# Mixture inputs as 128 and 64 rows, nine passes an expert, the inner remainder on POOL and row normalisation on ACT, in a vision transformer layer

## The chip, the cores and the metric

One core of one Trainium2 chip runs the whole program. Its engines are TensorE (PE), VectorE (DVE), ScalarE (ACT), GpSimd (POOL) and SyncE (SP, which only issues DMAs here); each takes its instructions in the order in which they are written, and engines wait for each other on semaphores. The metric is the device time of one execution in microseconds; smaller is better.

## The reference

The program is one layer of a vision transformer on 64 images of 3 x 224 x 224. Patch embedding gives 197 tokens of 192 features an image. Then comes attention with a residual, and then a mixture of experts with a residual, which is the part that the change touches:

```python
h = tok(x)                                   # 64 x 197 x 192
h = h + attn(layernorm(h))
y = layernorm(h)                             # rows of 192
scores = sigmoid(y @ gate_weight.T)          # 8 experts in 4 groups
# the best 2 groups, then the best 2 experts in them; their scores, normalised, are the weights cw
h1, h3 = y @ w1[e].T, y @ w3[e].T            # 192 -> 128, for each expert e
out = h + sum_e cw[e] * (silu(h1) * h3) @ w2[e].T + shared expert of the same shape
```

All 8 experts are computed for all tokens, with weight nought where an expert isn't chosen, and the shared expert is a ninth.

## The kernel before

The kernel has a set-up block and two phases. The set-up block loads the weights, and splits each into a high and a low part of 16 bits (`hi`, `lo`). Products use three passes, hi x hi, lo x hi and hi x lo, and leave lo x lo out. Phase A (embedding and attention) writes its tokens to DRAM; it isn't touched by the change.

Phase B is the mixture. It takes 12608 tokens in groups of 512 (4 lanes of 128 rows): 24 full groups and one of 320 (4 lanes of 80). For a group, `stats_of` (DVE) makes mean and variance of each row, `rstds` (POOL) the reciprocal square root, `normalise` (DVE) writes `bnorm`, `transposes` (PE) turn it into `ps_x`, `yT_out` splits it into `yT_hi` (ACT) and `yT_lo` (DVE), `gate` (PE) makes the scores, and `route` (DVE, five parts of small dependent steps) the weights `comb`. The 192 features lie as two chunks of 96 rows.

For each of the nine experts e of a group:

- `inner_products` (PE): for w1 and w3, two chunks and three passes of 512 columns, 12 matmuls, into `ps_h1` and `ps_h3` (two buffers each).
- `silu` (ACT) of ps_h1 into `act1`; `multiply` (DVE) by ps_h3 into `inner`; `inner_first` (ACT) rounds to `in_hi`; `inner_rest` (DVE) gives `in_lo` = inner - in_hi.
- `outer_products` (PE): 12 matmuls of 192 columns into `ps_y`, in two halves; each half waits until `accumulate` has read that half of the expert before, and the first waits for `in_lo`.
- `accumulate` (DVE) adds comb x ps_y to `acc`, four instructions (two for the shared expert, L1130).

The order is written out by hand. PE issues the inner products of e, then the outer products of e-2; after expert 3's it does the transposes of the following group, after expert 5's that group's gate. DVE issues multiply(e), inner_rest(e-1), accumulate(e-2), and then: routing parts 3 and 4 of the own group behind experts 0 and 1; of the following group `stats_of` behind 1, `normalise` behind 2, `yT_out` behind 4, routing parts 0 to 2 behind 6, 7 and 8. ACT issues silu(e), inner_first(e), and the following group's `yT_out` behind 3 and `gate_out` behind 5. POOL does only `rstds`, once a group. SP loads the group after the next and stores this one. `run` unrolls three groups, loops over pairs, and unrolls the last four.

PE's outer products of expert 0 thus stand behind the inner products of expert 2, and need in_lo(0) and the accumulation of the shared expert of the group before.

## Time and profile before

| | us |
|---|---|
| median of 3 runs | 2052.69 (2049.91 to 2053.3) |
| the profiled execution's own time | 2049.82 |
| its span, first to last instruction | 2047.9 |
| PE busy | 1920.0 (94%) |
| DVE busy | 1319.4 (64%) |
| ACT busy | 909.9 (44%) |
| POOL busy | 47.4 (2%) |
| mean granted TensorE clock | 0.982 |

The busy times are of the whole span; phase A takes the first half, phase B begins near 1116 us. PE's busy time overlaps its weight loads, and a matmul's record is longer than the time after which the next can start, so issue times are taken from start to start.

### The profile page before, as it was taken

How to read it: one execution, taken by the hardware profiler on the slowest of the kernel's cores; microseconds unless marked ns; L12 is line 12 of the kernel's file. 1: busy time of each engine (PE TensorE's matmuls, PEld its weight loads, DVE VectorE, ACT ScalarE, POOL GpSimd, SP SyncE). 2: the span in 40 equal slices, each digit the busy share in tenths (PEclk: the TensorE clock that was granted, in tenths of full speed). 3: DMA queues.
4: the chain of work that ended last, by engine and by line, in shares of the span. 5: the costliest groups of instructions: out<-in, count | busy, mean ns of one | idle time of the engine just before them, and what ended most of it. 6: DMA issues, size and time to landing. Idle time of an engine off the chain costs nothing. (4 is left out here: it accounts for less than half of the span.)

```text
span 2047.9 us, 47882 instructions
## 1 busy us (share of the span) xinstructions
PE 1920.0 (94%) x17848; PEld 1348.0 (66%) x17848; DVE 1319.4 (64%) x3554; ACT 909.9 (44%) x1878; POOL 47.4 (2%) x63
## 2 busy tenths in 40 slices
PE   3999999999999999999996999999999999999998
PEld 2777777777777777777774555555555555555556
DVE  3455545455454554544452888888888888888887
ACT  2555555555555555555553333333333333333332
POOL 0000000000000000000000000000000000000000
PEclk9999999999999999999996999999999999999999
DMA  4011111111111111111100000000000000000000
GB/s 152 17 46 50 57 47 46 48 46 46 48 46 47 47 59 35 55 53 47 46 23 28 17 24 17 31 15 15 31 15 23 23 15 31 15 23 23 16 21 14
DMA packets 31508, 74.73 MB, mean 36 GB/s; under 512 B 3435, under 2 KB 16366, under 8 KB 31214
## 3 DMA queue, kind: packets, MB, share of 16 engines
q1 hardware_dynamic: 31310, 72.10, 11.3%
q8 instruction: 123, 2.02, 0.4%
q14 instruction: 75, 0.61, 0.1%
HBM read 52.73 MB, written 19.37 MB: 35 GB/s over the span
## 5 line engine op out<-in xcount | busy, mean ns | idle before, releaser
L572 ACT ACTIVATE prob<-ps_sc 99x792 f32<-99x792 f32 x384 | 317.4, 827 | 109.4 <-PE ps_sc L413 90.8
L907 PE MATMUL ps_h<-yT_hi,w_hi 96*128 96x512 f16 (+1 forms) x900 | 341.2, 379 | 0.0
L909 PE MATMUL ps_h<-yT_lo,w_hi 96*128 96x512 f16 (+1 forms) x900 | 339.9, 378 | 0.0
L910 PE MATMUL ps_h<-yT_hi,w_lo 96*128 96x512 f16 (+1 forms) x900 | 339.7, 377 | 0.0
L357 PE MATMUL ps_hid<-lin_f,xin 128*99 128x192 f32 x1536 | 288.6, 332 | 32.5 <-DMA xin<-xp 29.2
L981 ACT ACTIVATE in_hi<-inner 128x512 f16<-128x512 f32 (+1 forms) x225 | 140.4, 624 | 337.9 <-DVE inner L1100 337.9
L357 PEld LDWEIGHTS ps_hid<-lin_f,xin 128*99 128x99 f32 x1536 | 243.3, 170 | 34.4 <-DMA xin<-xp 29.2
L925 PE MATMUL ps_y<-w_hi,in_hi 128*128 128x192 f16 (+1 forms) x900 | 222.3, 247 | 39.6 <-DVE acc L1124 28.0
L973 ACT ACTIVATE act<-ps_h 128x512 f32<-128x512 f32 (+1 forms) x225 | 132.3, 588 | 274.7 <-PE ps_h L910 274.0
L1124 DVE SCALAR_TENSOR_TENSOR acc<-ps_y,comb,acc 128x192 f32<-128x192 f32 (+1 forms) x700 | 242.3, 407 | 0.0
L1100 DVE SCALAR_TENSOR_TENSOR inner<-ps_h,act 128x512 f32<-128x512 f32 (+1 forms) x225 | 152.4, 677 | 125.4 <-ACT act L973 115.5
L927 PE MATMUL ps_y<-w_hi,in_lo 128*128 128x192 f16 (+1 forms) x900 | 221.1, 246 | 0.0
L926 PE MATMUL ps_y<-w_lo,in_hi 128*128 128x192 f16 (+1 forms) x900 | 220.9, 245 | 0.0
L413 PE MATMUL ps_sc<-qT,kT 32*99 32x198 f32 x3072 | 180.3, 349 | 6.4 <-DVE kT L676 1.8
L428 PE MATMUL ps_o<-prob,v 98*32 98x198 f32 (+1 forms) x3072 | 172.0, 342 | 12.5 <-ACT prob L572 8.1
L910 PEld LDWEIGHTS ps_h<-yT_hi,w_lo 96*128 96x128 f16 x900 | 88.1, 98 | 105.7 <-issue 3.2
L1106 DVE TENSOR_TENSOR in_lo<-inner,in_hi 128x512 f16<-128x512 f32 (+1 forms) x225 | 151.2, 672 | 0.0
L658 DVE TENSOR_REDUCE qk_var<-qk_sq 99x24 f32<-99x384 f32 x128 | 70.2, 549 | 125.2 <-ACT qk_sq L531 125.2
L925 PEld LDWEIGHTS ps_y<-w_hi,in_hi 128*128 128x128 f16 (+1 forms) x900 | 88.2, 98 | 90.9 <-DVE acc L1124 33.8
L413 PEld LDWEIGHTS ps_sc<-qT,kT 32*99 32x99 f32 x3072 | 116.4, 161 | 42.9 <-issue 16.3
L909 PEld LDWEIGHTS ps_h<-yT_lo,w_hi 96*128 96x128 f16 x900 | 88.7, 99 | 79.5 <-issue 1.9
L907 PEld LDWEIGHTS ps_h<-yT_hi,w_hi 96*128 96x128 f16 x900 | 88.2, 98 | 79.3 <-issue 2.4
(112 smaller groups left out, 3001.0 us busy)
## 6 DMA issues: line engine op xcount, KB each, us to landing
xin<-xp SPq DMA_DIRECT2D x64, 594.0 KB, 3.9
hidden_dram<-h SPq DMA_DIRECT2D x64, 147.0 KB
hin<-hidden_dram SPq DMA_DIRECT2D x24, 384.0 KB, 3.0
out<-acc SPq DMA_DIRECT2D x24, 384.0 KB, 2.3
w_f<-w SPq DMA_DIRECT2D x1, 1728.0 KB, 11.7
hidden_dram<-h SPq DMA_DIRECT2D x64, 0.8 KB
w_f<-w SPq DMA_DIRECT2D x1, 864.0 KB, 13.2
lin_f<-w_lin SPq DMA_DIRECT2D x1, 576.0 KB
```

The source lines that it names most:

```text
L357: last = pe.matmul(hid[:, t, :], xin[q][:, k, t * TR:(t + 1) * TR], lin_f[:, k, :], start=(k == 0), stop=(k == PCHUNKS - 1))
L413: last = pe.matmul(sc[:, place, m, :], kT[p][rows, quad, m * TR:(m + 1) * TR], qT[p][rows, quad, :], start=True, stop=True)
L428: last = pe.matmul(o_quad[VB * place:VB * place + VB, :], v[p][rows, m, QUAD * quad + place, :], prob[quad][rows, place, m, :], start=(m = ...
L572: act.activation(prob[quad][:, places].rearrange("p h m s -> p h (m s)"), ps_sc[0:TR, places, 0:2 * SLOTS], ACT.Exp, scale=D ** -0.5 / (SQ ...
L907: pe.matmul(bank[:, 0:N], w13_hi[:, k, e, w, :], yT_hi[p][:, k, 0:N], start=(k == 0), stop=False)
L909: pe.matmul(bank[:, 0:N], w13_hi[:, k, e, w, :], yT_lo[p][:, k, 0:N], start=False, stop=False)
L910: last = pe.matmul(bank[:, 0:N], w13_lo[:, k, e, w, :], yT_hi[p][:, k, 0:N], start=False, stop=(k == 1))
L925: pe.matmul(dst, in_hi[b][:, s], w2_hi[:, e, :], start=True, stop=False)
L926: pe.matmul(dst, in_hi[b][:, s], w2_lo[:, e, :], start=False, stop=False)
L927: last = pe.matmul(dst, in_lo[b][:, s], w2_hi[:, e, :], start=False, stop=True)
L1100: dve.scalar_tensor_tensor(out=inner[e % 3][:, 0:N], in0=ps_h3[b][:, 0:N], scalar=SA / SS, in1=act1[b][:, 0:N], op0=ALU.mult, op1=ALU.mult ...
L1124: last = dve.scalar_tensor_tensor(out=acc[p][0:R, t, :], in0=ps_y[half_no][0:R, u * C:(u + 1) * C], scalar=comb[p][0:R, t, e:e + 1], in1=b ...
```

## The change

- The 192 features of `yT_hi` and `yT_lo` lie as one chunk of 128 rows and one of 64. The 64 are held twice, in rows 0 to 63 and 64 to 127 of chunk 1. The host lays out w13 and the gate's weights alike (`tailed`).
- In chunk 1, rows 0 to 63 of `w13_hi` hold the high part and rows 64 to 127 the low part. One full matmul w13_hi x yT_hi on 128 rows makes hi x hi and lo x hi at once. The remaining hi x lo pass needs only 64 rows; `w13_lo` has the high part in rows 0 to 63 for w1 and in rows 64 to 127 for w3. So an expert has 2 x 4 full matmuls and two of 64 rows, on different rows of the array and into different banks.
- The gate has five matmuls a lane, where it had six.
- `inner_rest` goes from DVE to POOL, and waits for the silu of the next expert as well. In POOL's body, the following group's `rstds` come ahead of the remainder of expert 0.
- `normalise` goes from DVE to ACT, as eight activations a group with a scale and a bias for each row; `bnorm` is 256 wide, features 128 to 191 twice. Its two halves stand behind experts 1 and 2. POOL makes the bias from mean and reciprocal root, by two more instructions.
- `stats_of` moves from behind expert 1 to behind expert 0.
- In the set-up block w13 grows from 96 to 128 rows, and its low part is made by four instructions where it was one (the gate's too).

```diff
 # set-up block, DVE
+                        if f in tailed:
+                            dve.scalar_tensor_tensor(out=lo[:, 0], in0=f[:, 0], scalar=SW, in1=hi[:, 0],
+                                                     op0=ALU.mult, op1=ALU.subtract)
+                            dve.tensor_copy(lo[0:64, 1], hi[0:64, 1])
+                            dve.memset(lo[64:128, 1], 0.0)
+                            dve.scalar_tensor_tensor(out=hi[64:128, 1], in0=f[64:128, 1], scalar=SW, ...
+                        elif f is w13_f:
+                            dve.scalar_tensor_tensor(out=lo[:, 0], in0=f[:, 0], scalar=SW, in1=hi[:, 0], ...
+                            dve.tensor_copy(lo[0:64, 1, :, 0, :], hi[0:64, 1, :, 0, :])
+                            dve.tensor_copy(lo[64:128, 1, :, 1, :], hi[64:128, 1, :, 1, :]).then_inc(w_tail_done, 1)
+                            dve.wait_ge(w_tail_done, 1)
+                            dve.scalar_tensor_tensor(out=hi[64:128, 1], in0=f[64:128, 1], scalar=SW, ...
 # PE
             def transposes(g):
-                pe.wait_ge(bnorm_done, g.times(1, 1))
+                pe.wait_ge(bnorm_done, g.times(2, 2))
...
-                for k in range(2):
-                    for t in range(T):
-                        last = pe.transpose(ps_x[k][0:KC, t * R:(t + 1) * R], bnorm[0:R, t, k * KC:(k + 1) * KC],
-                                            id32[0:R, 0:R])
+                for t in range(T):
+                    s = slice(t * R, (t + 1) * R)
+                    for k in range(2):
+                        last = pe.transpose(ps_x[k][:, s], bnorm[0:R, t, k * 128:(k + 1) * 128], id32[0:R, 0:R])
             def gate(g):
...
-                    for k in range(2):
-                        pe.matmul(dst, yT_hi[p][:, k, s], gate_hi[:, k, :], start=(k == 0), stop=False)
-                        pe.matmul(dst, yT_hi[p][:, k, s], gate_lo[:, k, :], start=False, stop=False)
-                        last = pe.matmul(dst, yT_lo[p][:, k, s], gate_hi[:, k, :], start=False, stop=(k == 1))
+                    pe.matmul(dst, yT_hi[p][:, 0, s], gate_hi[:, 0], start=True, stop=False)
+                    pe.matmul(dst, yT_hi[p][:, 0, s], gate_lo[:, 0], start=False, stop=False)
+                    pe.matmul(dst, yT_lo[p][:, 0, s], gate_hi[:, 0], start=False, stop=False)
+                    pe.matmul(dst, yT_hi[p][:, 1, s], gate_hi[:, 1], start=False, stop=False)
+                    last = pe.matmul(dst, yT_lo[p][:, 1, s], gate_lo[:, 1], start=False, stop=True)
             def inner_products(g, e):
...
-                for w, bank in ((0, ps_h1[b]), (1, ps_h3[b])):
-                    for k in range(2):
-                        pe.matmul(bank[:, 0:N], w13_hi[:, k, e, w, :], yT_hi[p][:, k, 0:N],
-                                  start=(k == 0), stop=False)
-                        pe.matmul(bank[:, 0:N], w13_hi[:, k, e, w, :], yT_lo[p][:, k, 0:N], start=False, stop=False)
-                        last = pe.matmul(bank[:, 0:N], w13_lo[:, k, e, w, :], yT_hi[p][:, k, 0:N],
-                                         start=False, stop=(k == 1))
+                for w, bank in enumerate(banks):
+                    pe.matmul(bank, w13_hi[:, 0, e, w, :], y_hi[:, 0], start=True, stop=False)
+                    pe.matmul(bank, w13_hi[:, 0, e, w, :], y_lo[:, 0], start=False, stop=False)
+                    pe.matmul(bank, w13_lo[:, 0, e, w, :], y_hi[:, 0], start=False, stop=False)
+                    pe.matmul(bank, w13_hi[:, 1, e, w, :], y_hi[:, 1], start=False, stop=False)
+                for w, bank in enumerate(banks):
+                    rows = slice(64 * w, 64 * w + 64)
+                    last = pe.matmul(bank, w13_lo[rows, 1, e, w, :], y_lo[rows, 1], start=False, stop=True)
 # ACT
+            def normalise(g, half_no):
+                R, p = rows_of(g), g.mod(2)
+                act.wait_ge(bneg_done, g.times(1, 1))
+                if half_no == 0 and reached(g.times(1)):
+                    act.wait_ge(yT_done, g.times(1))
+                for t in (2 * half_no, 2 * half_no + 1):
+                    for dst, src in ((slice(0, C), slice(0, C)), (slice(C, 256), slice(128, C))):
+                        last = act.activation(bnorm[0:R, t, dst], hin[p][0:R, t, src], ACT.Identity,
+                                              scale=brstd[0:R, t:t + 1], bias=bshift[0:R, t:t + 1])
+                last.then_inc(bnorm_done, 1)
...
                     inner_first(g, e)
+                    if e in (1, 2) and following.active():
+                        normalise(following, e - 1)
 # DVE
                     multiply(g, e)
-                    if e > 0:
-                        inner_rest(g, e - 1)
-                    elif g.back(1).active():
-                        inner_rest(g.back(1), NE - 1)
...
                     if following.active():
-                        if e == 1:
+                        if e == 0:
                             stats_of(following)
-                        if e == 2:
-                            normalise(following)
 # POOL
                 pool.tensor_tensor(brstd[0:R], bvareps[0:R], minus_half[0:R], ALU.pow).then_inc(brstd_done, 1)
+                pool.wait_ge(brstd_done, g.times(1, 1))
+                settle(pool, settled)
+                pool.tensor_tensor(bshift[0:R], bmv[0:R, :, 0], brstd[0:R], ALU.mult).then_inc(bshift_done, 1)
+                pool.wait_ge(bshift_done, g.times(1, 1))
+                settle(pool, settled)
+                pool.tensor_scalar(bshift[0:R], bshift[0:R], -1.0, None, ALU.mult).then_inc(bneg_done, 1)
+            def inner_rest(g, e):
+                N, b = T * rows_of(g), e % 3
+                pool.wait_ge(inhi_done, g.times(NE, e + 1))
+                if e + 1 < NE or g.back(-1).active():
+                    pool.wait_ge(silu_done, g.times(NE, e + 2))
+                settle(pool, settled)
+                pool.tensor_tensor(in_lo[b][:, 0:N], inner[b][:, 0:N], in_hi[b][:, 0:N],
+                                   ALU.subtract).then_inc(inlo_done, 1)
...
             def body(g):
-                if g.back(-1).active():
-                    rstds(g.back(-1))
+                for e in range(NE):
+                    if e == 0 and g.back(-1).active():
+                        rstds(g.back(-1))
+                    inner_rest(g, e)
```

## Rows read from the trace of the kernel before

**Rows 1.** Windows, phase B: us, busy PE, PEld, DVE, ACT, POOL; clock, DMA.

```profile
1400.00:1600.00 200.00, 188.28 (x1341) 112.41 (x1342) 167.16 (x468) 64.50 (x114) 9.63 (x11) 0.98 0.06 22
```

**Rows 2.** The timeline of POOL, phase B: start, us, what, idle before.

```profile
1437.08 0.23 POOL L1179 TENSOR_SCALAR bvareps<-bmv 128x4 f32<-128x4 f32 x1 [36.39 <-DVE bmv L1010]
1437.39 1.56 POOL L1181 TENSOR_TENSOR brstd<-bvareps,minus_half 128x4 f32<-128x4 f32 x1
...
1991.00 0.22 POOL L1179 TENSOR_SCALAR bvareps<-bmv 80x4 f32<-80x4 f32 x1 [34.34 <-DVE bmv L1010]
```

**Rows 3.** The timeline of PE, one group of tokens; columns as before.

```profile
1426.27 0.25 PE L925 MATMUL ps_y<-w_hi,in_hi 128*128 128x192 f16 x1
...
1427.26 0.38 PE L907 MATMUL ps_h<-yT_hi,w_hi 96*128 96x512 f16 x1
...
1429.86 0.25 PE L925 MATMUL ps_y<-w_hi,in_hi 128*128 128x192 f16 x1
...
1433.93 0.26 PE L925 MATMUL ps_y<-w_hi,in_hi 128*128 128x192 f16 x1 [0.33 <-DVE acc L1130]
...
1438.77 0.26 PE L925 MATMUL ps_y<-w_hi,in_hi 128*128 128x192 f16 x1 [1.08 <-DVE acc L1124]
...
1440.58 1.08 PE L880 MATMUL ps_x<-id,bnorm 128*96 128x128 f32 x8 [0.49 <-DVE bnorm L1019]
```

**Rows 4.** The timeline of DVE in the same stretch.

```profile
1419.93 0.69 DVE L1100 SCALAR_TENSOR_TENSOR inner<-ps_h,act 128x512 f32<-128x512 f32 x1 [0.47 <-ACT act L973]
...
1423.76 0.69 DVE L1100 SCALAR_TENSOR_TENSOR inner<-ps_h,act 128x512 f32<-128x512 f32 x1 [0.20 <-DVE rank L1061]
...
1427.29 0.69 DVE L1100 SCALAR_TENSOR_TENSOR inner<-ps_h,act 128x512 f32<-128x512 f32 x1 [0.20 <-DVE masked L1080]
...
1428.50 1.39 DVE L1124 SCALAR_TENSOR_TENSOR acc<-ps_y,comb,acc 128x192 f32<-128x192 f32 x4
1429.80 0.41 DVE L1052 TENSOR_TENSOR cmp<-masked 128x256 f32<-128x256 f32 x1
...
1432.12 0.69 DVE L1100 SCALAR_TENSOR_TENSOR inner<-ps_h,act 128x512 f32<-128x512 f32 x1 [0.20 <-DVE rank L1061]
...
1433.33 1.01 DVE L1130 SCALAR_TENSOR_TENSOR acc<-ps_y,acc 128x384 f32<-128x384 f32 x2
...
1435.22 1.13 DVE L1006 BATCH_NORM_STATS2 bstats<-hin 128x6 f32<-128x192 f32 x4
```

**Rows 5.** The timeline of ACT, one expert.

```profile
1426.47 0.60 ACT L973 ACTIVATE act<-ps_h 128x512 f32<-128x512 f32 x1 [1.19 <-PE ps_h L910]
1428.10 0.63 ACT L981 ACTIVATE in_hi<-inner 128x512 f16<-128x512 f32 x1 [1.03 <-DVE inner L1100]
```

**Rows 6.** Timeline of PE, phase A: from full matmuls to 32-row ones.

```profile
613.63 0.25 PE L342 MATMUL ps_mix<-proj_hi,onT_lo 96*99 96x192 f16 x1
613.80 0.93 PE L413 MATMUL ps_sc<-qT,kT 32*99 32x198 f32 x16
614.66 0.37 PE L428 MATMUL ps_o<-prob,v 98*32 98x198 f32 x3
```

**Rows 7.** Grouped lines of ACT by shape: count, busy us, mean ns, idle.

```profile
L543 ACT ACTIVATE qk_lnvar<-qk_var,eps_qk 99x24 f32<-99x24 f32 x128 | 40.2, 314 | 91.6 <-DVE qk_var L658 91.6
...
L546 ACT ACTIVATE qk_rstd<-qk_lnvar 99x24 f32<-99x24 f32 x128 | 28.5, 223 | 4.1
```

**Rows 8.** The timeline of POOL in the first microseconds.

```profile
0.83 1.41 POOL L226 MEMSET qk_norm<- 99x768 f32 x2
```

**Rows 9.** The timeline of PE around the gating products.

```profile
1412.33 0.17 PE L892 MATMUL ps_x<-gate_hi,yT_hi 96*128 96x8 f16 x1
...
1412.93 0.38 PE L907 MATMUL ps_h<-yT_hi,w_hi 96*128 96x512 f16 x1
```

**Rows 10.** The windows view over four microseconds at the low clock.

```profile
1402.00:1406.00 4.00, 3.61 (x13) 2.28 (x14) 2.76 (x7) 1.71 (x3) 0.00 (x0) 0.57 0.33 98
```

**Rows 11.** The timeline of DVE in the set-up block.

```profile
17.95 6.82 DVE L217 SCALAR_TENSOR_TENSOR w_lo<-w_f,w_hi 96x4608 f16<-96x4608 f32 x2 [6.44 <-ACT w_hi L199]
```

More of the change, by code:

```diff
@@ L123, in vit_layer @@
             proj_hi, proj_lo = split_pair("proj", [KC, 2, C])
-            gate_hi, gate_lo = split_pair("gate", [KC, 2, EXPERTS])
-            w13_hi, w13_lo = split_pair("w13", [KC, 2, NE, 2, INTER])
+            gate_hi, gate_lo = split_pair("gate", [128, 2, EXPERTS])
+            w13_hi, w13_lo = split_pair("w13", [128, 2, NE, 2, INTER])
             w2_hi, w2_lo = split_pair("w2", [INTER, NE, C])
@@ L216, in _ @@
                         dve.wait_ge(w_hi_done, n + 1)
-                        dve.scalar_tensor_tensor(out=lo[:], in0=f[:], scalar=SW, in1=hi[:],
-                                                 op0=ALU.mult, op1=ALU.subtract).then_inc(w_lo_done, 1)
+                        if f in tailed:
[3 more added lines that the diff above has]
+                            dve.memset(lo[64:128, 1], 0.0)
+                            dve.scalar_tensor_tensor(out=hi[64:128, 1], in0=f[64:128, 1], scalar=SW,
+                                                     in1=hi[64:128, 1], op0=ALU.mult,
+                                                     op1=ALU.subtract).then_inc(w_lo_done, 1)
+                        elif f is w13_f:
+                            dve.scalar_tensor_tensor(out=lo[:, 0], in0=f[:, 0], scalar=SW, in1=hi[:, 0],
+                                                     op0=ALU.mult, op1=ALU.subtract)
+                            dve.tensor_copy(lo[0:64, 1, :, 0, :], hi[0:64, 1, :, 0, :])
+                            dve.tensor_copy(lo[64:128, 1, :, 1, :], hi[64:128, 1, :, 1, :]).then_inc(w_tail_done, 1)
+                            dve.wait_ge(w_tail_done, 1)
+                            dve.scalar_tensor_tensor(out=hi[64:128, 1], in0=f[64:128, 1], scalar=SW,
+                                                     in1=hi[64:128, 1], op0=ALU.mult,
+                                                     op1=ALU.subtract).then_inc(w_lo_done, 1)
+                        else:
+                            dve.scalar_tensor_tensor(out=lo[:], in0=f[:], scalar=SW, in1=hi[:],
+                                                     op0=ALU.mult, op1=ALU.subtract).then_inc(w_lo_done, 1)
                 @block.gpsimd
@@ L769, in phase_b @@
         brstd = sb("brstd", [128, T])
-        bnorm = sb("bnorm", [128, T, C])
-        yT_hi = [sb(f"yT_hi{p}", [KC, 2, GT], F16) for p in range(2)]
-        yT_lo = [sb(f"yT_lo{p}", [KC, 2, GT], F16) for p in range(2)]
+        bshift = sb("bshift", [128, T])
+        bnorm = sb("bnorm", [128, T, 256])
+        yT_hi = [sb(f"yT_hi{p}", [128, 2, GT], F16) for p in range(2)]
+        yT_lo = [sb(f"yT_lo{p}", [128, 2, GT], F16) for p in range(2)]
         act1 = [sb(f"act1{p}", [INTER, GT]) for p in range(2)]
@@ L956, in yT_out @@
                 for k in range(2):
-                    act.activation(yT_hi[p][:, k, 0:N], ps_x[k][0:KC, 0:N], ACT.Copy,
+                    act.activation(yT_hi[p][:, k, 0:N], ps_x[k][:, 0:N], ACT.Copy,
                                    scale=SX).then_inc(yThi_done, 1)
@@ L983, in _ @@
             first = Index(0, 0, 2, GROUPS_B)
+            normalise(first, 0)
+            normalise(first, 1)
             yT_out(first)
@@ L1010, in stats_of @@
                     dve.bn_aggr(bmv[0:R, t, :], bstats[0:R, t, :]).then_inc(bmv_done, 1)
-            def normalise(g):
-                R, p = rows_of(g), g.mod(2)
-                dve.wait_ge(brstd_done, g.times(1, 1))
-                if reached(g.times(1)):
-                    dve.wait_ge(yT_done, g.times(1))
-                for t in range(T):
-                    last = dve.tensor_scalar(bnorm[0:R, t, :], hin[p][0:R, t, :], bmv[0:R, t, 0:1],
-                                             brstd[0:R, t:t + 1], ALU.subtract, ALU.mult)
-                last.then_inc(bnorm_done, 1)
             def yT_out(g):
@@ L1026, in yT_out @@
                     dve.wait_ge(yThi_done, g.times(2, k + 1))
-                    dve.scalar_tensor_tensor(out=yT_lo[p][:, k, 0:N], in0=ps_x[k][0:KC, 0:N], scalar=SX,
+                    dve.scalar_tensor_tensor(out=yT_lo[p][:, k, 0:N], in0=ps_x[k][:, 0:N], scalar=SX,
                                              in1=yT_hi[p][:, k, 0:N], op0=ALU.mult,
@@ L1101, in multiply @@
                                          in1=act1[b][:, 0:N], op0=ALU.mult, op1=ALU.mult).then_inc(mul_done, 1)
-            def inner_rest(g, e):
-                N, b = T * rows_of(g), e % 3
-                dve.wait_ge(inhi_done, g.times(NE, e + 1))
-                dve.tensor_tensor(in_lo[b][:, 0:N], inner[b][:, 0:N], in_hi[b][:, 0:N],
-                                  ALU.subtract).then_inc(inlo_done, 1)
             def accumulate(g, e):
@@ L1136, in _ @@
             stats_of(first)
-            normalise(first)
             yT_out(first)
```

19 lines of the change are left out of this document (13 added, 6 removed).

## The prediction

> **What bounds the kernel now.** I read the windows view first. In phase B a 200-us stretch has PE busy for 188 and DVE for 167, at a granted clock of 0.98, while ACT has 64.5 and POOL under 10 [rows 1]. PE is nearly full and DVE is close behind; the reader should ask where each ends the wait. The timeline of POOL gives the length of one group of 512 tokens, because its reciprocal square root runs once a group: 1437.08 to 1991.00 us is 15 groups, 36.93 us each [rows 2]. The timelines of PE and DVE then show one group from inside. An expert's outer products take 0.99 us of issue (1426.27 to 1427.26) and its inner products 2.60 (to 1429.86), so PE needs 3.59 an expert [rows 3]. It stalls in three places of the group, always for DVE: 0.33 for the shared expert's accumulation, 1.08 for the next one, 0.49 for the normalised rows ahead of the transposes [rows 3]. They follow experts 0 and 1, where DVE has the large routing part (1429.80 to 1432.12, 2.32 us) and the statistics (from 1435.22) on top of its usual work [rows 4]. So PE's columns bound most of a group, and DVE's queue bounds the stretch around experts 0 to 3. Phase A is not touched.
>
> **The sum, part by part.** I number the experts of a group 0 to 8 and write P(e) for the moment at which PE has issued the inner products of expert e. The method is to walk one group queue by queue. Checked on the kernel before: PE's outer products of expert 0 need the first half of the shared expert's accumulation, which starts at 1433.33 and takes 0.5; PE starts at 1433.93 [rows 3, 4]. The walk holds there to 0.1 us.
>
> *Nine passes.* Twelve 512-column matmuls took 2.60, 0.216 each [rows 3]. Eight remain full, and two use 64 rows each, on different rows and banks. Phase A shows such packing: 16 matmuls of 32 rows take 0.86 us (613.80 to 614.66), 0.054 each, against 0.082 for one 192-column matmul of the outer products (0.99/12), so they overlap; going in costs 0.17 minus 0.08, 0.09 [rows 3, 6]. I price the pair at 0.216, plus 0.09, plus about 0.07 for its stagger and the way out (bounds 0 and 0.3 for the three together): 2.10 for the inner products, 3.09 for an expert's step. The transposes' weights grow from 96 to 128 columns: between 1.08 [rows 3] and 4/3 of it, I take 1.25. The gate's 24 products took 0.60 [rows 9]; 20 take 0.50.
>
> *The inner remainder moves to POOL.* DVE loses one of two equal halves of 1428.50 minus 1427.29, 0.60 an expert [rows 4]. POOL gains it. No long POOL subtraction is in the trace. From below it is DVE's 0.60; a memset of 768 elements takes about 0.70, so two input streams of 512 take 0.93, with 0.23 for a tiny operation 1.1, and with a third stream for the output 1.6 [rows 2, 8]. I take 1.1. The Trainium skill, GPSIMD Engine Reference, section 3.1, puts two-input arithmetic at 2.6 cycles an element at 1.2 GHz, and calls ordinary elementwise work the wrong use of this engine; that would be an estimated 1.11 plus dispatch, and the sum would stay. In a usual step it is hidden: silu(e+1) starts 0.20 behind P(e+1) and takes 0.60 [rows 3, 5], so POOL ends near P(e+1)+1.95, and PE wants the result only at P(e+2), that is P(e+1)+3.09. Above 2.2 us the cover is gone.
>
> *Row normalisation on ACT.* DVE loses four instructions a group, and PE its 0.49 wait. ACT gains eight. A 24-element one takes 0.22, an operand per row adds 0.09 [rows 7], and the slope to the 0.60 of 512 elements [rows 5] gives, with two such operands, 0.53 for 192 and 0.43 for 64 elements: 1.9 a half group, less what back-to-back instructions overlap. I take 1.6 (bounds 1.4 and 1.9). ACT has 135 of 200 us free [rows 1]. In experts 1 and 2 silu stands behind it; the walk below shows whether that hurts.
>
> *The queue of POOL.* This is the step I weigh most. In a group's body POOL first issues the next group's rstds, and only then the remainder of expert 0. The rstds wait for the statistics, which now stand at the end of DVE's expert 0. Behind them wait in_lo(0), then PE's outer products of expert 0, then all of PE. Walk from P(0)=0. silu(0) ends and DVE's multiply starts at 0.82; the accumulation at 1.42 and takes 1.30 (1428.50 to 1429.80), so routing starts at 2.72, and 2.32 later, at 5.04, the statistics [rows 4]. POOL's first instruction follows the start of the statistics by 1.86 (1435.22 to 1437.08): 6.90 [rows 2, 4]. It and the power take 1.87 (0.31 and 1.56); the two added small ones, each with its wait, 0.31 each: 9.39 [rows 2]. in_lo(0) ends at 10.54, and PE can go on at 10.64. PE itself is there at P(2)=6.18. **A new stall of 4.5 us replaces the 1.9 of before.**
>
> *The rest of the group.* P(3)=13.73. ACT normalises until 11.0, silu(2) ends at 11.6, in_lo(1) at 12.8: in time for 13.73. The second half ends near 14.65, the transposes are due at 14.72: in time, 0.6 late at worst. in_lo(2) ends near 16.4 against P(4)=18.07. Later DVE is the shorter queue: the step from multiply 7 to multiply 8 was 3.83 and becomes 3.23, that to the next group's 3.53 becomes 2.93 [rows 4], against 3.09 of PE; the 0.14 over is absorbed. So after 10.64 PE issues seven outer sets (6.93), seven inner sets (14.70), the transposes (1.25) and the gate (0.50): the period is 34.0.
>
> *The clock.* After such stalls the granted clock fell in places: 1402 to 1406 ran at 0.57, with PE at the lower of its two levels (1.2 instead of 2.4 GHz) for most of it [rows 10]. That is 43% of 4 us, 1.7 lost. The 0.98 of the long stretch is 4 us lost in 200, so two such falls in some five groups [rows 1, 2]; their cost is in the 36.93. With PE idle for 4.5 us in a row in every group I expect one such fall in each; part of it lies in the idle time, some last longer: 1.6 a group (bounds 0 and 3.3). Period 35.6.
>
> *Sum.* 36.93 minus 35.6 is 1.3 us, times 24 periods, 32 us. Once only: the larger first and second matrices in the set-up block, where two DVE instructions took 6.82 [rows 11] and three more come, with a third more bytes ahead of them, cost 2 to 5, I take 3.5; the first group's normalisation has nothing to hide under: ACT's 3.2 and POOL's 0.62 for DVE's 1.2, 2.5; the short last group gains some 2. Net 4. So 28 us off. Against its own profiled time of 2049.8 that is 2021.8; the median of the runs is 2.9 above that execution, so I forecast **2025**. Anything within 0.2% (4 us) of 2052.7 is what a measurement can't tell from no change.
>
> **Rivals.**
> 1. *The clock holds* through the stalls, as in most groups of before. Period 34.0: 2.9 times 24, less 4, gives 1987. Against: the stalls of before were 0.3 to 1.1 long, this one 4.5 [rows 3].
> 2. *The POOL queue doesn't bind,* since DVE is ready earlier or POOL's chain is shorter beside other work. PE then waits only for the shared expert's accumulation, near 7.8: period 31.2, 1920. Against: the power alone takes 1.56 [rows 2].
> 3. *On the other side: POOL and DVE block each other.* The subtraction runs beside multiply and accumulate. If each holds DVE for its whole 1.1, expert 0 ends 1.1 later, and four other steps that carry routing or yT_lo run over by about 0.8: 4.3 a group, 2128. From 0.3 us of blocking an instruction on the kernel is slower. For: nothing in the trace has a long POOL operation beside DVE. Against: the power ran beside multiply, and DVE's spacing stood [rows 2, 4], though it reads four elements. The Trainium skill, SBUF — State Buffer, "Who interferes with whom", lets only DVE instructions with two SBUF inputs (or in a two-port mode) collide with a reading POOL; here DVE reads PSUM and one SBUF operand, so by that rule the blocking is nought where in_lo runs.
> 4. *The low clock lasts twice as long* in each group: 1.7 more, 2066.
> 5. *The pair does not overlap,* ten passes and not nine: seven times 0.216, 1.5 a group, 2061. Against: rows 6.
>
> **How the numbers follow.** Main case 0.54, with 2004 to 2045 as its own range (the bounds of clock, pair and subtraction each moving it by part of their width); rival 1 0.14, rival 2 0.08, rival 3 0.09, rival 4 0.08, rival 5 0.07. Range 1980 to 2066: it leaves out rival 2, rival 3 and little else. Faster 0.75, same 0.03, slower 0.22.
>
> **What would show it.** One long idle stretch of PE in each group, ahead of the outer products of expert 0, released by POOL's in_lo; POOL starts about 34 to 36 us apart; the step of PE near 3.09; the subtraction near 1.1; DVE under 0.75 busy; ACT near 75 of 200 us; the granted clock of phase B near 0.95. The forecast is wrong if the stall is short or split, if the subtraction or DVE's instructions stretch when they meet, or if the clock stays at 1.00.

## The result and the profile after

The changed kernel takes 2020.7 us (median; 2018.69 to 2022.14) against 2052.5 for the kernel before (2049.91 to 2053.3) on the same chip: ratio 0.9852, 95% interval 0.9831 to 0.9873. So it is 32 us, 1.5%, faster, which is clear of the noise. The forecast was 2025. The profiled execution spans 2019.0 us.

The page shows where to look first, in its parts 4 and 5: a wait of TensorE for POOL, which the kernel before did not have. Columns of a group: line, engine, operation, operands, count; busy us, mean ns; idle us just before and what ended most of it.

```profile
PE 28%; DVE 8%; POOL 3%; issue 3%; ACT 1%; DVEq 0%; POOLq 0%; DMA 0%; ACTq 0%
...
L1215 POOL TENSOR_TENSOR in_lo<-inner,in_hi 128x512 f16<-128x512 f32 (+1 forms) x225 | 257.9, 1146 | 457.3 <-ACT act L1014 449.1
L954 PE MATMUL ps_y<-w_hi,in_hi 128*128 128x192 f16 (+1 forms) x900 | 234.3, 260 | 97.8 <-POOL in_lo L1215 94.1
```

The windows view of phase B answers to [rows 1] (columns as there; the second line is the stretch of [rows 1]):

```profile
1200.00:1400.00 200.00, 176.19 (x1232) 101.86 (x1231) 138.31 (x420) 85.58 (x164) 67.59 (x74) 0.92 0.07 24
1400.00:1600.00 200.00, 180.37 (x1290) 104.21 (x1289) 140.04 (x421) 83.45 (x159) 67.69 (x71) 0.93 0.06 20
```

PE is busy for less of the time (176 and 180 of 200 us against 188), DVE for much less (138 and 140 against 167), POOL does seven times its old work and ACT 30% more. No engine is full: a wait now sets the pace. The granted clock is 0.92 to 0.93 where it was 0.98.

The timeline of POOL gives the period, as in [rows 2]:

```profile
1173.29 0.23 POOL L1199 TENSOR_SCALAR bvareps<-bmv 128x4 f32<-128x4 f32 x1 [4.69 <-DVE bmv L1055]
...
1388.65 0.23 POOL L1199 TENSOR_SCALAR bvareps<-bmv 128x4 f32<-128x4 f32 x1 [4.97 <-DVE bmv L1055]
1388.96 1.04 POOL L1201 TENSOR_TENSOR brstd<-bvareps,minus_half 128x4 f32<-128x4 f32 x1
1390.17 0.20 POOL L1204 TENSOR_TENSOR bshift<-bmv,brstd 128x4 f32<-128x4 f32 x1 [0.18 <-POOL brstd L1201]
1390.57 0.24 POOL L1207 TENSOR_SCALAR bshift<-bshift 128x4 f32<-128x4 f32 x1 [0.20 <-POOL bshift L1204]
1390.85 1.15 POOL L1215 TENSOR_TENSOR in_lo<-inner,in_hi 128x512 f16<-128x512 f32 x1
...
1959.89 0.22 POOL L1199 TENSOR_SCALAR bvareps<-bmv 80x4 f32<-80x4 f32 x1 [4.70 <-DVE bmv L1055]
```

From 1173.29 to 1959.89 are 22 groups, 35.75 us each; most single ones alternate between 35.06 and 36.6. Inside a group, POOL sits idle for 4.97 us until DVE's statistics arrive, works through four small instructions in 2.2 us, and only then begins the remainder of expert 0. PE shows the price:

```profile
1381.56 0.26 PE L954 MATMUL ps_y<-w_hi,in_hi 128*128 128x192 f16 x1
...
1387.52 0.39 PE L940 MATMUL ps_h<-yT_lo,w_lo 64*128 64x512 f16 x2
1392.13 0.34 PE L954 MATMUL ps_y<-w_hi,in_hi 128*128 128x192 f16 x1 [4.21 <-POOL in_lo L1215]
...
1394.02 0.63 PE L933 MATMUL ps_h<-yT_hi,w_hi 128*128 128x512 f16 x1
```

The first of these rows is P(0) of the prediction's walk, so PE resumes at P(0)+10.57 (1392.13); the walk said 10.64. The outer set behind the stall takes 1.89 us of issue (1392.13 to 1394.02) instead of 0.99. The windows view says why (columns as in [rows 1]):

```profile
1391.00:1392.00 1.00, 0.00 (x0) 0.00 (x0) 0.00 (x0) 1.00 (x3) 1.00 (x1) 0.93 0.98 390
1392.00:1395.00 3.00, 2.87 (x15) 2.23 (x16) 1.83 (x5) 2.08 (x6) 1.16 (x1) 0.50 0.00 1
1395.00:1396.00 1.00, 1.00 (x6) 0.39 (x5) 0.16 (x1) 1.00 (x4) 0.00 (x0) 0.87 0.00 0
```

The granted clock is at its lower level, 1.2 of 2.4 GHz, just when PE has work again. In the next group, whose stall is 3.74 us, it stays there longer:

```profile
1428.00:1432.00 4.00, 4.00 (x15) 1.97 (x14) 1.99 (x5) 2.20 (x6) 1.16 (x1) 0.50 0.16 28
```

That is the alternation of the periods: every second group pays for about twice as long a stretch.

DVE's part of the walk, to be held against [rows 4]:

```profile
1382.62 0.69 DVE L1134 SCALAR_TENSOR_TENSOR inner<-ps_h,act 128x512 f32<-128x512 f32 x1 [0.65 <-ACT act L1014]
1383.22 1.39 DVE L1152 SCALAR_TENSOR_TENSOR acc<-ps_y,comb,acc 128x192 f32<-128x192 f32 x4
1384.52 0.41 DVE L1086 TENSOR_TENSOR cmp<-masked 128x256 f32<-128x256 f32 x1
...
1386.78 1.14 DVE L1051 BATCH_NORM_STATS2 bstats<-hin 128x6 f32<-128x192 f32 x4
```

The accumulation still takes 1.39. The statistics start at P(0)+5.22 (the walk: 5.04).

### The profile page after: what moved, and what is told of

Same layout as the page of the kernel before. It is cut to its first block and busy times, and to the rows that moved or that the text cites. A ratio compares the mean times of both kernels' runs of the same rounds, so it can differ in the third digit from the quotient of the medians.

```text
span 2019.0 us, 47371 instructions
## 1 busy us (share of the span) xinstructions
PE 1845.4 (91%) x17298; PEld 1288.7 (64%) x17298; DVE 1167.5 (58%) x3235; ACT 990.2 (49%) x2078; POOL 303.3 (15%) x338
## 5 line engine op out<-in xcount | busy, mean ns | idle before, releaser
L1215 POOL TENSOR_TENSOR in_lo<-inner,in_hi 128x512 f16<-128x512 f32 (+1 forms) x225 | 257.9, 1146 | 457.3 <-ACT act L1014 449.1
L954 PE MATMUL ps_y<-w_hi,in_hi 128*128 128x192 f16 (+1 forms) x900 | 234.3, 260 | 97.8 <-POOL in_lo L1215 94.1
L956 PE MATMUL ps_y<-w_hi,in_lo 128*128 128x192 f16 (+1 forms) x900 | 232.8, 259 | 0.0
L955 PE MATMUL ps_y<-w_lo,in_hi 128*128 128x192 f16 (+1 forms) x900 | 232.7, 259 | 0.0
L1199 POOL TENSOR_SCALAR bvareps<-bmv 128x4 f32<-128x4 f32 (+1 forms) x25 | 5.7, 227 | 1240.8 <-DVE bmv L1055 1240.8
L933 PE MATMUL ps_h<-yT_hi,w_hi 128*128 128x512 f16 (+1 forms) x450 | 179.1, 398 | 0.0
L934 PE MATMUL ps_h<-yT_lo,w_hi 128*128 128x512 f16 (+1 forms) x450 | 178.8, 397 | 0.0
L935 PE MATMUL ps_h<-yT_hi,w_lo 128*128 128x512 f16 (+1 forms) x450 | 178.1, 396 | 0.0
L936 PE MATMUL ps_h<-yT_hi,w_hi 128*128 128x512 f16 (+1 forms) x450 | 176.4, 392 | 0.0
L698 DVE COPY kT<-ps_mix 128x297 f32<-128x297 f32 x128 | 59.2, 462 | 121.7 <-PE ps_mix L421 121.7
```

The source lines that it names most:

```text
L933: pe.matmul(bank, w13_hi[:, 0, e, w, :], y_hi[:, 0], start=True, stop=False)
L934: pe.matmul(bank, w13_hi[:, 0, e, w, :], y_lo[:, 0], start=False, stop=False)
L935: pe.matmul(bank, w13_lo[:, 0, e, w, :], y_hi[:, 0], start=False, stop=False)
L936: pe.matmul(bank, w13_hi[:, 1, e, w, :], y_hi[:, 1], start=False, stop=False)
L954: pe.matmul(dst, in_hi[b][:, s], w2_hi[:, e, :], start=True, stop=False)
L955: pe.matmul(dst, in_hi[b][:, s], w2_lo[:, e, :], start=False, stop=False)
```

## The experiments

My theory: the period is PE's work, plus one stall in which PE waits for POOL's first remainder (held up by the statistics on DVE and by POOL's four small instructions, `rstds`), plus the low clock behind that stall. The rivals at this point: POOL and DVE slow each other down; or the gain is that of one part alone and the rest of the change does nothing.

### The POOL order

The remainder of expert 0 goes ahead of the chain of the next group's statistics:

```
-                    if e == 0 and g.back(-1).active():
-                        rstds(g.back(-1))
                     inner_rest(g, e)
+                    if e == 0 and g.back(-1).active():
+                        rstds(g.back(-1))
```

> The changed kernel with one swap in POOL's body: the following group's rstds stand behind the remainder of expert 0, not ahead of it. Theory (POOL's queue order sets the stall): PE goes on with the outer products of expert 0 when the shared expert's accumulation has freed ps_y, some 8.0 us behind P(0) where it was 10.6. But ACT's first half of the normalisation still waits for the rstds (ready at 9.3), and holds silu(2) and with it in_lo(1): a second stall of about 1.7, a third of 0.8 ahead of the transposes. Period 34.2 to 35.2 us where the changed kernel has 35.75; time 1984 to 2008, likeliest 1995. Rival (the order is harmless, DVE's queue alone sets the stall): no change, 2021 within 4.

Measured 1984.9 us, ratio 0.9682 (0.9652 to 0.9711); from 1175.95 to 1924.95 are 22 groups of 34.05. The wait for in_lo(0) is gone from the waits view of PE; what is left are DVE's accumulations and a little of ACT (1200 to 1900 us; total us, times, longest us):

```profile
PE ps_y L954 <- DVE acc L1158: 37.3, 21, 2.6
PE ps_y L954 <- DVE acc L1152: 21.9, 13, 1.8
PE ps_x L905 <- ACT bnorm L990: 7.3, 20, 0.4
```

So the order of two calls on POOL cost 36 us. The time is at the fast end of what was expected, because the second stall isn't what I took it for: I had ACT at 1.7 us a group, and it is 0.4 at the longest. The next stall in line belongs to DVE, where routing and statistics still stand together.

### Statistics a group earlier

The statistics go two groups ahead, behind expert 5 on DVE, where I expected room; POOL's chain goes behind its remainder of expert 5, and the prologue makes the second group's statistics too.

```
-                    if e == 0 and g.back(-1).active():
-                        rstds(g.back(-1))
                     inner_rest(g, e)
+                    if e == 5 and g.back(-2).active():
+                        rstds(g.back(-2))
...
-                        if e == 0:
-                            stats_of(following)
...
+                    if e == 5 and g.back(-2).active():
+                        stats_of(g.back(-2))
```

> The changed kernel with the statistics and rstds of the group after the next made behind expert 5, a group ahead of their use, so that neither POOL nor ACT waits for them behind experts 0 to 2; in the prologue the second group's are made too. Theory (PE is bound by its columns once the wait is gone): period 9 x 3.15 for the experts, 0.9 for the transposes, 0.5 for the gate, under 1 of stalls: 30.0 to 31.0 us, the clock at 1.00, time 1885 to 1910, likeliest 1890. Rival (DVE is the bound behind it, since its load in experts 7 to 1 passes PE's step): period above 32, time above 1930.

Measured 1912.9 us, ratio 0.9321 (0.9292 to 0.9351), a little above the expected 1885 to 1910. The period is 31.29 ((1847.12 - 1158.66)/22); the clock of phase B is 1.00 and PE is busy for 192 of 200 us. Here single groups alternate too, 30.85 and 32.20, and the timeline of DVE shows something that the theory did not have:

```profile
1418.88 0.42 DVE L1088 TENSOR_TENSOR eq<-eq,bef 128x256 f32<-128x256 f32 x1
1419.34 1.35 DVE L1092 TENSOR_TENSOR cmp<-cmp,eq 128x256 f32<-128x256 f32 x1
1420.72 0.42 DVE L1095 TENSOR_REDUCE rank<-cmp 128x32 f32<-128x256 f32 x1
```

The same comparison took 0.42 us in the changed kernel. POOL at that moment:

```profile
1419.25 1.16 POOL L1217 TENSOR_TENSOR in_lo<-inner,in_hi 128x512 f16<-128x512 f32 x1 [1.99 <-ACT act L1014]
```

It holds from 1419.25 to 1420.41, and the comparison ends 0.28 us after that. Both operands of the comparison lie in SBUF. So the mechanism of rival 3, that the two block each other, exists, though not for the instructions that it named: multiply and accumulate keep their 0.69 and 1.39 beside POOL's subtraction, here and in the changed kernel.

### POOL without its wait for the next activation

```
                 pool.wait_ge(inhi_done, g.times(NE, e + 1))
-                if e + 1 < NE or g.back(-1).active():
-                    pool.wait_ge(silu_done, g.times(NE, e + 2))
```

The subtraction then runs directly behind in_hi, beside the routing part of DVE. This asks whether the collision has a price.

> The changed kernel without POOL's wait for the next expert's silu ahead of the inner remainder; in_hi's own wait stays. in_lo(e) then runs from P(e)+2.3 beside the accumulation and, behind experts 4 and 6 to 8, beside DVE's further instructions. Theory (POOL and DVE's instructions with two inputs in SBUF hold each other up, as one 1.35-us cmp with 0.42 of work suggests in the kernel with early statistics): routing instructions of 1.0 to 1.5 us appear behind experts 7 and 8, some in_lo above 1.16, but DVE has slack there: time 2018 to 2035, likeliest 2024. Rival (no holding up): all durations stay as they are and the time stays within 4 of 2021, or falls a little.

Measured 2059.7 us, ratio 1.0042 (1.0024 to 1.0061): 39 us above the changed kernel. The instructions that stretched are those expected (timeline of DVE):

```profile
1389.91 0.89 DVE L1100 TENSOR_SCALAR score<-half 128x32 f32<-128x32 f32 x1
...
1393.35 0.94 DVE L1086 TENSOR_TENSOR cmp<-gsum 128x64 f32<-128x64 f32 x1
...
1397.30 0.89 DVE L1107 TENSOR_SCALAR chosen<-rank 128x16 f32<-128x16 f32 x1
```

They take 0.16 to 0.22 otherwise; the subtraction itself stays at 1.15. The first runs beside the in_lo of 1389.61, the second beside that of 1393.05, the third beside that of 1397.00. The size was missed: 0.7 us on DVE three times a group was expected to cost little, since I counted slack on DVE that it does not have there. The waits view (1200 to 1900 us) shows 88.1 us for in_lo in 19 times, 4.7 at the longest, where the changed kernel has 78.9 in 20, 4.2 at the longest, and a new 8.7 for accumulations in 18; the clock fell to 0.90. So the wait for the activation is worth 39 us. What it prevents are these meetings: it puts the subtraction beside DVE's multiply and accumulate, which read PSUM. That these meetings make up the 39 us is argued; no run separates them from what else the wait does. The Trainium skill, SBUF — State Buffer, "Who interferes with whom", says that DVE instructions with two SBUF inputs or in a two-port mode collide with a reading POOL and others do not. The runs agree: the comparison has two SBUF inputs, and multiply and accumulate have one. The stretched tensor_scalar instructions have one too, and no run shows in which mode they ran.

### The collision in the early version taken away

Expert 0's remainder waits for the routing step behind the comparisons, not for silu(1):

```
+                if e == 0:
+                    pool.wait_ge(route_step, g.times(19, 15))
-                if e + 1 < NE or g.back(-1).active():
+                elif e + 1 < NE or g.back(-1).active():
                     pool.wait_ge(silu_done, g.times(NE, e + 2))
```

> The kernel with early statistics, and the remainder of expert 0 on POOL waits for the end of the ranks of 8 on DVE (routing step 15) in place of silu(1). Theory (the 0.93 us that the cmp behind expert 0 loses to in_lo(0) is most of the 1.1 us stall of PE behind it): all cmp instructions at 0.42, period 30.4 where early_stats has 31.3, time 1891 (1885 to 1900). Rival (in_lo(0) now ends later and takes the place of the stall): 1905 to 1913.

Measured 1910.0 us, ratio 0.9314 (0.9294 to 0.9334): the theory's 1885 to 1900 was missed. All comparisons take 0.42 again, but the period fell only from 31.29 to 30.95 and not to 30.4, since the collision had hit only every second group. The time lies in the rival's range, yet its mechanism isn't there: in all of phase B PE waits for in_lo only 3 times, 1.4 us together. To tell the two kernels apart I timed them again, side by side in five rounds.

> The same kernel as early_stats, timed again next to early_route on one chip, since their times so far (1912.9 and 1910.0) come from different ones. Expected 1910, 1905 to 1916.

> The same kernel as early_route. Its period of a group was 30.95 us against 31.29, so over 24 groups it should stand 5 to 8 us below early_stats on the same chip, at about 1903. If the order of the few POOL instructions around the routing does not matter outside one profiled execution, the two agree within 3 us.

Measured 1913.7 (1907.42 to 1916.46) and 1910.4 (1905.79 to 1913.99). The medians differ by 3 us both times, in the expected direction and below the expected 5 to 8, and the ranges overlap; the spans of these two profiled executions even stand the other way (1905.6 and 1908.6). The traces show why the totals can't decide it. From POOL's first instruction of phase B to the end of the span it is 792.3 us against 784.5 here (1113.31 to 1905.6, and 1124.11 to 1908.6), and 792.4 against 784.5 in the pair before (1122.26 to 1914.7, and 1117.05 to 1901.5). So removing the collision makes phase B 8 us shorter, twice. But phase B began 11 us apart in the two kernels timed side by side, though what runs before it is the same.

### Fill matmuls in the stall

Sixteen matmuls, whose result nobody reads, go behind the inner products of expert 2, where PE would stand idle:

```
                     inner_products(g, e)
+                    if e == 2:
+                        fill(g)
...
+                for _ in range(16):
+                    pe.matmul(ps_x[1][:], w13_hi[:, 0, 0, 0, :], yT_hi[p][:, 0], start=True, stop=True)
```

> The changed kernel with 16 more 512-column matmuls (1.73 us in the even half, 3.46 us in all) into ps_x[1], which nobody reads, issued by PE where it would stand idle for 4.2 us, ahead of the outer products of expert 0. The output is unaffected. Theory (the clock's share of the period is real): the granted clock of phase B comes to 0.99 or more, the outer and inner products behind the stall take 4.1 us where they take 4.7 to 5.6, period 34.2 where it is 35.75, time 1985 (1978 to 1998), although PE does more. Rival (the fall costs nothing because ACT's normalisation is late next anyway): 2012 to 2021. If the fills are on the path: above 2021.

Measured 1975.0 us, ratio 0.9625 (0.9605 to 0.9646), a little below the expected 1978 to 1998, with a period of 33.69. The timeline and the windows of this kernel:

```profile
1379.33 0.39 PE L940 MATMUL ps_h<-yT_lo,w_lo 64*128 64x512 f16 x2
1379.65 3.63 PE L962 MATMUL ps_x<-yT_hi,w_hi 128*128 128x512 f16 x16
1383.94 0.25 PE L954 MATMUL ps_y<-w_hi,in_hi 128*128 128x192 f16 x1 [0.66 <-POOL in_lo L1222]
```

```profile
1400.00:1600.00 200.00, 197.52 (x1434) 112.00 (x1432) 148.14 (x448) 89.24 (x173) 71.67 (x77) 1.00 0.07 24
```

PE waits for in_lo(0) just as long (1379.65 to 1383.94 is 4.29), but the clock stays at 1.00, and a group is 2.06 us shorter. That is the clock's share of the changed kernel's period; the stall itself (3.7 to 4.3) comes on top of it.

### The pair of 64-row matmuls one after the other

Both matmuls of 64 rows now use rows 0 to 63, so that they should not run beside each other; the same products are summed.

```
-                    rows = slice(64 * w, 64 * w + 64)
+                    rows = slice(0, 64)
```

> The changed kernel with both 64-row matmuls of an expert on rows 0 to 63 (one more half copied in the set-up block, 1 us once), so that they can't run beside each other; the same products are summed. Theory (the pair overlaps, nine passes): each inner set grows by 0.19 to 0.22, seven a group lie on the path: 1.3 to 1.5 us a group, time 2053 (2045 to 2060). Rival (the pair never overlapped, ten passes in effect): 2022 within 4.

Measured 2049.7 us, ratio 0.9981 (0.9968 to 0.9994), 29 us above the changed kernel; the period is 36.77. So in the change the pair does overlap, and its ninth pass is one pass and not two. The period grew by 1.0, less than the 1.5 of rival 5. Of nine times 0.22 the part ahead of the stall goes into the stall, whose mean over the 22 groups fell from 3.92 to 3.44 (longest: 4.2 and 3.7); that leaves 1.5. Most of the other 0.5 is the clock: one minus the granted clock, summed over windows of one microsecond, comes to 2.48 us a group in the changed kernel and to 2.09 here.

### Each part of the change alone

The nine passes with remainder, normalisation and statistics on DVE as before:

```
                     multiply(g, e)
+                    if e > 0:
+                        inner_rest(g, e - 1)
...
-                        if e == 0:
+                        if e == 1:
                             stats_of(following)
+                        if e == 2:
+                            normalise(following)
```

> One part alone: the 128/64 row layout and nine passes, while inner_rest, the normalisation (now eight DVE instructions) and the statistics stay on DVE where the kernel before has them. Theory (DVE's queue then binds): DVE's steps from expert 3 to 2 sum to 33.1 us, and it waits 1.4 and 0.6 for PE behind the transposes and the gate: period 35.1, time 2008 (1985 to 2025), so most of the change's gain, or more than it. Rival (the gain needs DVE's relief): within 10 us of the kernel before. The power on POOL should take 1.56 again if it is DVE's subtraction beside it that stretches it from 1.04.

Measured 2060.9 us, ratio 1.0046 (1.003 to 1.0062): a little slower than before, where I had expected 2008. The period is 37.52. The windows view of phase B and of five microseconds in it, and then PE's timeline:

```profile
1400.00:1600.00 200.00, 170.23 (x1184) 94.02 (x1183) 169.82 (x489) 63.65 (x112) 10.73 (x12) 0.95 0.06 22
...
1405.00:1410.00 5.00, 4.52 (x15) 2.77 (x16) 2.85 (x8) 1.72 (x3) 0.00 (x0) 0.50 0.15 57
```

```profile
1402.70 0.26 PE L954 MATMUL ps_y<-w_hi,in_hi 128*128 128x192 f16 x1 [1.63 <-DVE acc L1165]
...
1405.48 1.97 PE L905 MATMUL ps_x<-id,bnorm 128*128 128x128 f32 x8 [1.46 <-DVE bnorm L1146]
```

DVE had 167 of 200 us before and has 170 of 200 now, of a longer period: its queue is not shorter, and the normalisation, now split into eight instructions by the new layout, takes 2.13. PE's saving turns into waits for DVE (1.30, 1.63 and 1.46 ahead of three sets). Behind them the clock is at 0.50 for over five microseconds, the transposes take 1.97 instead of 1.1, and DVE then stands idle for 4.22 us for a silu that is late. My expectation had the DVE queue but a clock cost as before.

The two moves with the old layout and twelve passes (the same functions on POOL and ACT, 96 rows):

> The other part alone: inner_rest on POOL, normalisation on ACT, statistics behind expert 0, all as in the changed kernel, with the 96-row layout and twelve passes of the kernel before. Theory: the chain statistics, rstds, in_lo(0) ends at P(0)+10.6 as in the changed kernel, then PE issues seven inner sets of 2.60: period 37.4, and 1 to 1.7 for the clock: slower than before, 2075 to 2105, likeliest 2095. Rival (the moves relieve DVE and are worth having by themselves): 2030 or less.

Measured 2103.8 us, ratio 1.0266 (1.0234 to 1.0298), period 39.10, at the upper end of what was expected. Its waits view (1200 to 1900 us) has PE waiting for POOL's in_lo 18 times, 54.4 us in all, 3.2 at the longest. The stall is there without the passes, and nothing pays for it.

So neither part gains by itself as it is placed here: +8 us for the passes, +51 for the moves, -32 for both. The passes are worth 83 us once the moves have taken DVE's queue out of the way (2103.8 to 2020.7), and cost 8 without them.

### Were the passes alone held back by the clock?

Seven fill matmuls ahead of the outer products behind expert 3 and six ahead of the transposes, in the kernel of the passes alone.

> The kernel passes_alone (nine passes, all else on DVE as before) with 13 more 512-column matmuls a group into ps_x[1], which nobody reads: 7 ahead of the outer products issued behind expert 3, where PE stood idle for 1.6 us, and 6 ahead of the transposes, where it stood for 1.5. The output is unaffected. passes_alone had a period of 37.5 us where its DVE queue by itself asks for 35.1. Theory (the stalls in a row bring the clock down, and the slow transposes and inner products make DVE wait 4.2 us in place of 1.4): granted clock of phase B 0.99, that wait below 2, period 35.0 to 35.6, time 2010 (2000 to 2020). Rival (DVE's queue asks for 37.5 by itself, the clock is beside the point): 2055 or more.

Measured 2032.9 us, ratio 0.9902 (0.9877 to 0.9928): between the two theories' values. The timeline of PE, and one line of DVE's:

```profile
1394.66 1.69 PE L962 MATMUL ps_x<-yT_hi,w_hi 128*128 128x512 f16 x7
1396.36 0.26 PE L954 MATMUL ps_y<-w_hi,in_hi 128*128 128x192 f16 x1
...
1397.52 1.46 PE L962 MATMUL ps_x<-yT_hi,w_hi 128*128 128x512 f16 x6
1399.13 1.09 PE L905 MATMUL ps_x<-id,bnorm 128*128 128x128 f32 x8 [0.16 <-DVE bnorm L1154]
```

```profile
1395.57 1.39 DVE L1173 SCALAR_TENSOR_TENSOR acc<-ps_y,comb,hin 128x192 f32<-128x192 f32 x4
```

The clock is 1.00 throughout and the period 36.13 ((1973.27 - 1178.31)/22), 1.4 below the passes alone. That much was the clock. But DVE is busy for 178 of 200 us. The fills don't hold PE up: it goes on 0.79 us behind the start of the accumulation that its outer products need (1395.57 to 1396.36), as it did without fills in the passes alone (1401.91 to 1402.70). PE still waits for accumulations (0.59 and 1.30 ahead of this stretch, where no fills stand). With the clock repaired, the passes alone are worth 20 us; DVE's queue, which those waits point to, takes the rest.

### The moves and early statistics with twelve passes

> The kernel moves_alone (twelve passes, inner remainder on POOL, normalisation on ACT) with the early statistics of early_stats, so without the stall behind rstds. Theory (the moves relieve DVE, and PE's columns bind again): nine steps of 3.58, 1.1 for the transposes, 0.6 for the gate, 0.5 of stalls: period 34.4, clock 1.00, time 1990 (1980 to 2000). Against early_stats the three passes are then worth 3.1 us a group, 76 us in all, where without the moves they were worth nothing. Rival (the passes don't matter once the stall is gone, DVE or POOL binds both): within 15 us of 1913.

Measured 1973.9 us, ratio 0.9621 (0.959 to 0.9652), 16 below the expected middle. The windows view:

```profile
1400.00:1600.00 200.00, 200.00 (x1478) 124.38 (x1476) 147.82 (x443) 82.16 (x149) 72.15 (x78) 1.00 0.07 24
```

PE is busy for all of the 200 us; from the second period on, all are 33.72 to 33.74. This is what PE's work alone takes with twelve passes, and I had allowed for stalls that are not there. Against the same kernel with nine passes (31.29, of which some 1.3 are waits) the passes are worth 2.4 us a group, 61 in all, and not the 76 that I had expected. And the moves with twelve passes and early statistics gain 80 us (2053.5 to 1973.9), where with the statistics in the change's place they lost 51. What early statistics would give without the moves was not run, so the 80 can't be divided between the two.

## Why the prediction was right, point by point

**The place of the new stall.** Right, and shown: undoing the order on POOL removes it and 36 us. It comes once a group, ahead of the outer products of expert 0, released by POOL.

**Its size.** Predicted 4.5, measured 3.7 to 4.2. DVE's statistics came 0.2 later than in the walk, POOL's chain was 0.3 shorter. The power took 1.04 us and not the 1.56 of [rows 2]. In [rows 2] it ran beside DVE's in_lo, which reads two SBUF operands:

```profile
1437.38 0.68 DVE L1106 TENSOR_TENSOR in_lo<-inner,in_hi 128x512 f16<-128x512 f32 x1
```

After the change its neighbour on DVE is the accumulation of the shared expert (from 1388.97), with one operand in PSUM. In the passes alone, with in_lo back on DVE, it took 1.56 again. I had taken a duration from a row without asking what stood beside it, and the trace before had the other value, in the first group, where DVE ran nothing beside it:

```profile
1121.66 1.04 POOL L1181 TENSOR_TENSOR brstd<-bvareps,minus_half 128x4 f32<-128x4 f32 x1
```

**Nine passes.** The step of PE is 3.14 (1405.46 to 1408.60 from one inner set to the next), predicted 3.09. The two 64-row matmuls wait 0.10 to get in and are through 0.32 after that, against my 0.38 for all of it. The transposes, for which I took 1.25, issue in 0.87. There I had started from the 1.08 of their record, where start to start was 0.91 in the kernel before (1440.58 to 1441.49). The errors cancel in part. That the pair overlaps was rival 5's question, and the serial pair answered it.

**The subtraction.** Predicted 1.1, measured 1.15 (mean of 225). It is covered in the usual steps, as the walk had it: PE waits for it once a group and no more. ACT's normalisation takes 1.65 and 1.63 a half, predicted 1.6. ACT is busy for 84 to 86 of 200 us and not near 75; the prediction's own terms (64.5 a stretch before, 3.2 more a group) already give some 84.

**The clock.** This term was the least known, 1.6 us a group with bounds 0 and 3.3. The fills measured it: 2.06, with a granted clock of 0.92 to 0.93 where I had said near 0.95. It alternates, near 1.4 in one group and 2.9 in the next (periods 35.06 and 36.6 against 33.69).

**The period.** Predicted 34.0 without the clock and 35.6 with it; measured 33.69 and 35.75.

**Once only.** I took 3.5 us for the larger set-up block. In fact its last DVE instruction ended a microsecond earlier than before, at 23.8 against 24.77, for the transfer of the first matrix landed after 9.5 us and not 11.7, though it carries 2304 KB instead of 1728. So this term had the wrong sign: it was put at +3.5 and is about -1, 4.5 us too much. The first group's wait for its normalised rows grew from 10.8 to 13.4 us, 2.6, as forecast (2.5). The gain of 2 for the short last group isn't there: from POOL's first instruction of phase B to the end it is 926.6 us before and 901.4 after, 25.1 less, and 24 periods give 28.4 (36.96 less 35.77, from the second group on), so phase B has 3.3 of costs that come once, of which the 2.6 is the only one known.

**The closeness of the total.** That the forecast came within 4.3 us of the measured time is luck in part. The change in phase B (25.1) and the set-up block (1) give 26 us, near the forecast 28; the measured medians differ by 32. The rest falls ahead of phase B, where the two kernels are the same but for the set-up block, and where executions differ: phase B began at 1113.31 us in one run and at 1125.16 in another of the same set-up block and phase A.

**The rivals.** The clock does not hold (1), the queue of POOL binds (2), the pair overlaps (5), and the low clock lasts longer than I took it for, by 0.5 and not by 1.7 (4). Rival 3 is the instructive one. POOL and DVE do hold each other up, DVE by 0.7 to 0.9 us at a time, but in these runs only where DVE reads two SBUF operands or runs a plain tensor_scalar from SBUF. The prediction had set against it that the power ran beside multiply and that DVE's spacing stood. That was a misreading: it ran beside in_lo, and it was POOL that lost half a microsecond. In the changed kernel the wait for the next activation keeps such instructions away from the subtraction; taking it away cost the whole gain. The change came with this wait, so rival 3 did not come true here.

**The size of the gain.** The change takes a good deal of work off PE and DVE, and gives most of it back: 36 us to POOL's order, and to the statistics' place, with the order, 108 (2020.7 to 1912.9). The clock's 2.06 us a group, 46 in the run with fills, lies inside that, since it goes with the stall. The version with early statistics beats both kernels, at 0.932 of the kernel before.

## What to carry to other kernels

Before work moves to an idle engine, walk that engine's queue: a short chain that used to wait there harmlessly now stands ahead of something that the busiest engine needs. Two changes can each be worth nothing alone and a lot together, where each takes away the bound that hides the other, so time all four combinations; and where one of them loses, look for the stall that its order makes before giving it up, for the moves lost 51 us with the one place of the statistics and gained 80 with the other. And a stall on PE costs more than its length: look at the granted clock of the microseconds behind it, and put the cause out of the way before trimming columns.

## What the runs showed of the hardware that I had not expected

- A POOL subtraction of 512 elements a partition (1.15 us) holds up DVE instructions that read SBUF alone: a 0.42 us comparison took 1.35, one of 0.22 took 0.94, and a tensor_scalar of 32 elements took 0.89 instead of 0.17. POOL was not slowed in these. DVE's scalar_tensor_tensor with one input in PSUM kept its 0.69 beside the same subtraction.
- It also goes the other way: POOL's power on four elements a partition took 1.56 beside DVE's subtraction from SBUF, and 1.04 beside an accumulation from PSUM or alone.
- A larger transfer landed earlier: 2304 KB in 128 rows in 9.5 us, 1728 KB in 96 rows in 11.7. It holds in every trace: 9.0 to 10.4 in the eleven kernels with the larger one, 11.5 to 12.1 in the three with the smaller. The cause is open.
- The low clock does not last longer behind the longer stall: with a stall of 4.2 us it lasted some 3 us (from just before 1392 to past 1395), with the next group's 3.7 us over 6 (1426 to near 1432.7), again and again in turn. Why it alternates stays open.
- What runs before phase B took up to 12 us more or less from one execution to the next (start of phase B: 1113.31 to 1125.16 us). The granted clock from 600 to 1100 us goes with it: 0.99 in the execution with 1113.31, 0.97 in those with 1124.11 and 1125.16. Meanwhile phase B itself agreed within 0.1 us in two executions of one kernel (792.4 and 792.3, and 784.5 twice).
